# One of sixteen states is scaled by C on GpSimd and summed on TensorE, in a state-space layer with a routed feed-forward part

## What is computed

```python
u     = conv4(h) + conv_b                      # causal, per channel
dt, Bm, Cm = split(u @ xproj_w.T)              # 128, 16 and 16 columns
delta = softplus(dt @ dtproj_w.T + dtproj_b)
h_n[t] = exp(delta[t] * A_n) * h_n[t-1] + delta[t] * Bm[t, n] * u[t]
y[t]   = sum_n h_n[t] * Cm[t, n] + u[t] * D_skip
x1     = x + ga * y
```

## Time and profile before

| | |
|---|---|
| median of 3 runs | 1313.03 us (1310.49 to 1315.65) |
| the profiled execution | 1310.42 us, of which the span is 1308.7 us |
| PE busy | 1120.7 us, 86% of the span |
| DVE busy | 1110.2 us, 85% |
| POOL busy | 916.8 us, 70% |
| ACT busy | 877.6 us, 67% |
| granted PE clock, mean | 0.929 of full speed |

### The profile page before, as it was taken

How to read it: one execution, slowest core, us unless ns; L and a number is a source line. 1 busy time by engine, 2 the same in 40 slices (tenths; PEclk the granted TensorE clock), 3 DMA queues, 4 the chain that set the end, 5 groups by cost and what they waited for, 6 DMA issues and landing times. The chain is left out here.

```text
span 1308.7 us, 19847 instructions
## 1 busy us (share of the span) xinstructions
PE 1120.7 (86%) x5556; PEld 753.5 (58%) x5556; DVE 1110.2 (85%) x1562; ACT 877.6 (67%) x1684; POOL 916.8 (70%) x788
## 2 busy tenths in 40 slices
PE   8979778767769988898889998989889698999994
PEld 4467655445546656565557674656566465666551
DVE  4898899999988999899789998999889998853145
ACT  4864887948658975897598669976788474453231
POOL 2576686788778878888898767988887877423211
PEclk9999969757979999999999998999999789999997
DMA  6576443123224325233444521442541345785575
GB/s 213 182 262 218 121 158 101 49 73 139 82 93 121 129 66 153 94 130 96 140 119 132 145 64 60 143 137 72 155 121 66 115 143 183 232 285 185 153 232 171
DMA packets 104739, 181.02 MB, mean 138 GB/s; under 512 B 24864, under 2 KB 33056, under 8 KB 103608
## 3 DMA queue, kind: packets, MB, share of 16 engines
q1 hardware_dynamic: 91432, 141.33, 35.2%
q0 software_dynamic: 13200, 38.43, 7.7%
HBM read 116.34 MB, written 68.86 MB: 142 GB/s over the span
## 5 line engine op out<-in xcount | busy, mean ns | idle before, releaser
L1247 POOL TENSOR_TENSOR DB<-DU,BR 128x1024 f32<-128x1024 f32 x222 | 523.3, 2365 | 125.2 <-DVE H L1677 107.8
L2014 PE MATMUL pb<-ID,H 128*128 128x128 f32 x2048 | 323.8, 294 | 86.8 <-DVE ACC L1702 63.5
L1465 ACT ACTIVATE pb<-DELP,AN 128x512 f32<-128x512 f32 x448 | 305.7, 687 | 135.5 <-DVE H L1677 127.0
L1702 DVE SCALAR_TENSOR_TENSOR ACC<-pb,CTM,ACC 128x512 f32<-128x512 f32 x512 | 373.5, 730 | 13.9 <-PE pb L2014 13.4
L2014 PEld LDWEIGHTS pb<-ID,H 128*128 128x128 f32 x2048 | 254.2, 151 | 173.5 <-DVE ACC L1702 67.6
L1677 DVE TENSOR_TENSOR_SCAN H<-pb,DB 128x512 f32<-128x512 f32 x256 | 310.9, 1215 | 35.1 <-ACT pb L1465 17.3
L1677 DVE TENSOR_TENSOR_SCAN H<-pb,ST,DB 128x512 f32<-128x512 f32 x192 | 244.9, 1275 | 12.4 <-ACT pb L1465 9.1
L1232 POOL DMA_INDIRECT ydr<-YO,SCR x85 | 89.9, 1058 | 145.6 <-ACT YO L1547 129.7
L1547 ACT ACTIVATE YO<-pb,SCR 128x512 f32<-128x512 f32 x85 | 58.1, 683 | 71.5 <-PE pb L2117 71.1
L2087 PE MATMUL pb<-WU,XTS 128*128 x340 | 99.5, 417 | 0.0
L2112 PE MATMUL pb<-WD,GT 128*128 x170 | 98.4, 661 | 0.0
(11 more groups left out here) (251 smaller groups left out, 1731.9 us busy)
## 6 DMA issues: line engine op xcount, KB each, us to landing
BR<-bscr SPq DMA_DIRECT2D x112, 256.0 KB
XS<-xdr SPq DMA_DIRECT2D x85, 256.0 KB
DU<-ydr SPq DMA_DIRECT2D x64, 256.0 KB
xdr<-ZZ SPq DMA_DIRECT2D x37, 264.0 KB, 5.3
ACC<-in_x SPq DMA_DIRECT2D x16, 512.0 KB, 3.5
DU<-in_x SPq DMA_DIRECT2D x7, 1024.0 KB, 5.6
x1s<-ACC SPq DMA_DIRECT2D x24, 256.0 KB, 2.2
DELP<-x1s SPq DMA_DIRECT2D x24, 256.0 KB, 3.5
```

The lines of the kernel that those rows point to most:

```text
L1247: eng.tensor_tensor(DB[:, i % NDB:i % NDB + 2], DU[:, c % 2, r:r + 2], BR[:, n % 2:n % 2 + 1].to_broadcast([128, 2, CT]), ALU.mult).then_i ...
L1465: eng.activation(DA[i % NDA][:], DEL[:, c % 2, r], ACT.Exp, scale=AN[:, r, n:n + 1]).then_inc(S["da"], 1)
L1702: eng.scalar_tensor_tensor(out=acc, in0=banks[bank_of["flip", c, n, r]][:], scalar=1.0 if n < 0 else CTM[:, c % 2, j, st:st + 1], in1=acc, ...
L2014: t = eng.transpose(b[:, dt * 128:dt * 128 + 128], src[:, dt, r * 128:r * 128 + 128], ID[:])
```

## The change

In the chunks 1 to 6 the state 1 no longer goes through its own four flips and four accs. Instead the row of C for that state is written to HBM (`cw`, 512 single elements) and read back as a broadcast row CR (`cr`); POOL multiplies the state in H by it, in two instructions of 128x1024 (`hs`); and each of the four flips of the skip term becomes eight matrix products with the identity, four of U and four of the scaled state, added in the PSUM bank. The four accs of the skip term then add both. The skip flips of these chunks wait for both `hs`, and the scan of state 4 now waits for the last skip flip.

The expert rows' places XS go from 4 to 3, which gives the room for CR. The back phase gets four pairs of places for the rows and eight for x1; the new ones lie where chunk 7 has its own DU and DEL, and are free only when chunk 7 has made its last use of them. The acc of state 0 now also waits for the second half of the accumulator's load (`d_xa1`).

The tables PLACES and BANKS are replaced as a whole. The numbers that matter below, before and after: the skip flips of chunk c at 2048c+104 to 2048c+127, then at 2048c+327 to 2048c+430 (chunk 7 as before), and the skip accs at 2048c+121 to 2048c+144, then at 2048c+373 to 2048c+493; the new `hs` at 2048c+201 to +272 in the chunks 1, 2, 3 and 5 and at 2048c+312 and +333 in the chunks 4 and 6; `gbk` (five small POOL instructions on GBC) at 1106, then -30, just ahead of the dbu of slot 2; the load of the second half of ACC for chunk 6 at 12166, then 12440 (its first acc has 12530); of the expert tiles' `dn`, 40 have numbers below 14336 (chunk 7) before and 39 after, of the `up` 44 and 42, of the `xt` 46 and 42.

```diff
+FOLD = (1,)
...
-NXS = 4
+NXS = 3
...
+def folded(c, n):
+
+    return n in FOLD and c > 0 and c not in SPLIT
+
+
+def folding(c):
+
+    return folded(c, FOLD[0])
...
+    for c in filter(folding, range(NC)):
+        at += [("cw", c)] + [("cr", c, n) for n in FOLD] + [("hs", c, n, r) for n in FOLD for r in (0, 2)]
...
-        at += [(32 * s, ("scan", *unit(s))), (32 * (s + LAG) + 1, ("flip", *unit(s))), (32 * (s + LAG) + 50, ("acc", *unit(s)))]
+        at.append((32 * s, ("scan", *unit(s))))
+        if not folded(*unit(s)[0:2]):
+            at += [(32 * (s + LAG) + 1, ("flip", *unit(s))), (32 * (s + LAG) + 50, ("acc", *unit(s)))]
...
+        CR = sb("CR", [128, len(FOLD), CT])
...
+        cscr = nc.dram_tensor("cscr", [NC, len(FOLD), CT], f32).ap()
...
+        def x1_chunk(r):
+
+            return NC - 2 if r < 4 else NC - 1
+
+        def z_chunk(r):
+
+            return NC - 2 if r < 2 else NC - 1
+
         def x1_tile(g, t):
 
             cs, j = tokens(g)[t]
             if not bounced(cs):
                 return acc_tile(cs // 2, 2 * (cs % 2) + j)
-            return DEL[:, (NC - 2) % 2, back_no(g, t) % 4]
+            r = back_no(g, t) % 8
+            return DEL[:, x1_chunk(r) % 2, r % 4]
 
         def z_tile(g, t, way):
 
-            return DU[:, (NC - 2) % 2, 2 * (back_no(g, t) % 2) + way]
+            r = back_no(g, t) % 4
+            return DU[:, z_chunk(r) % 2, 2 * (r % 2) + way]
 
 
         def turn_of_z(g, t):
 
-            return S[f"d_g{back_no(g, t) % 2}"], back_no(g, t) // 2
+            return S[f"d_g{back_no(g, t) % 4}"], back_no(g, t) // 4
 
 
         def turn_of(g, t):
 
             r = back_no(g, t)
-            return S[f"d_v{r % 4}"], S[f"d_p{r % 4}"], r // 4
+            return S[f"d_p{r % 8}"], sum(32 if x < 4 * (NC - 2) else 16 for x in range(r % 8, r, 8))
...
+                elif what == "cw":
+                    c = k[0]
+                    eng.wait_ge(S["bct"], c + 1)
+                    eng.wait_ge(S["dts"], c + 1)
+                    for i, n in enumerate(FOLD):
+                        eng.dma_start(cscr[c, i].rearrange("(j p) -> p j", p=128), CTM[:, c % 2, :, n],
+                                      allow_slow_non_contiguous=True).then_inc(S["d_cw"], 16)
+                elif what == "cr":
+                    c, n = k
+                    i = FOLD.index(n)
+                    eng.wait_ge(S["d_cw"], 16 * len(FOLD) * c)
+                    if c > 1:
+                        eng.wait_ge(S["hs"], 2 * (len(FOLD) * (c - 2) + i + 1))
+                    eng.dma_start(CR[:, i], cscr[c, i:i + 1, :].to_broadcast([128, CT])).then_inc(S["d_cr"], 16)
...
-                        eng.wait_ge(S["fin"], b - 1)
+                        eng.wait_ge(S["fin"], b - 3)
                     elif way == 0:
-                        eng.wait_ge(S["dbu"], slot(NC - 2, NS - 1, 3) + 1)
+                        eng.wait_ge(S["dbu"], slot(z_chunk(b), NS - 1, 3) + 1)
...
-                    loaded, stored, turn = turn_of(g, t)
-                    if turn:
-                        eng.wait_ge(stored, 16 * turn)
+                    moved, before = turn_of(g, t)
+                    if before:
+                        eng.wait_ge(moved, before)
                     else:
-                        eng.wait_ge(S["da"], slot(NC - 2, NS - 1, 3) + 1)
+                        eng.wait_ge(S["da"], slot(x1_chunk(back_no(g, t)), NS - 1, 3) + 1)
                     eng.wait_ge(S[f"d_x1{2 * (cs % 2) + j}"], 16 * (cs // 2 + 1))
-                    eng.dma_start(x1_tile(g, t), x1s[rows_of(g, t), :]).then_inc(loaded, 16)
+                    eng.dma_start(x1_tile(g, t), x1s[rows_of(g, t), :]).then_inc(moved, 16)
...
+                elif what == "hs":
+                    c, n, r = k
+                    i = FOLD.index(n)
+                    eng.wait_ge(S["scan"], slot(c, n, r + 1) + 1)
+                    if state_kept(c, n):
+                        eng.wait_ge(S["st"], nth["st", c, n])
+                    eng.wait_ge(S["d_cr"], 16 * (len(FOLD) * (c - 1) + i + 1))
+                    h = H[:, (c * NS + n) % NH, r:r + 2]
+                    eng.tensor_tensor(h, h, CR[:, i:i + 1].to_broadcast([128, 2, CT]), ALU.mult).then_inc(S["hs"], 1)
...
-                        eng.wait_ge(S["flip"], nth["flip", pc, pn, 3])
+                        eng.wait_ge(S["flip"], nth["flip", pc, -1, SKIP[-1]] if folded(pc, pn) else nth["flip", pc, pn, 3])
...
+                        eng.wait_ge(S["d_xa1"], 16 * (c + 1))
...
+                    if n < 0 and r == 2 and folding(c):
+                        eng.wait_ge(S["hs"], 2 * len(FOLD) * c)
                     b = work_bank(eng, task)
                     src = U if n < 0 else H[:, (c * NS + n) % NH]
-                    for dt in range(4):
+                    parts = [U] + [H[:, (c * NS + x) % NH] for x in FOLD] if n < 0 and folding(c) else []
+                    for dt in range(4 if parts else 0):
+                        for x, part_of in enumerate(parts):
+                            t = eng.matmul(b[:, dt * 128:dt * 128 + 128], part_of[:, dt, r * 128:r * 128 + 128], ID[:],
+                                           start=x == 0, stop=x == len(parts) - 1)
+                    for dt in range(0 if parts else 4):
                         t = eng.transpose(b[:, dt * 128:dt * 128 + 128], src[:, dt, r * 128:r * 128 + 128], ID[:])
```

More of the change, by code:

```diff
@@ L38 @@
 PLACES = {
-        "del": (11, 17, 1852, 1865, 1916, 1942, 3384, 3394, 3516, 3529, 5944, 5954, 6008, 6018, 7995, 8005, 8077, 8131, 9973,
[5 rows of a table removed]
[L45 to L50, removed]
-        "bdh": (147,),
[L52 to L57, removed]
@@ L230 @@
-        "out": (15832, 15864, 16023, 16166, 16413, 16479, 16541, 16606, 16750, 16839, 16928, 17036, 17144, 17267, 17346, 17472,
[5 rows of a table removed]
+        "del": (-3, -2, 1852, 1865, 1938, 1979, 3706, 3714, 3738, 3853, 6005, 6012, 6018, 6025, 8050, 8056, 8074, 8080, 10101,
[5 rows of a table added]
+        "gbt": (176,),
+        "gbm": (11,),
+        "gbk": (-30,),
+        "gbb": (1233,),
+        "gbe": (1274,),
+        "gbs": (1340,),
+        "bdh": (147,),
+        "bdl": (176,),
+        "gbl": (1507, 1514, 16610, 17638),
+        "dg2": (12,),
@@ new lines @@
+        "rowz": (227, 242),
+        "rowy": (231, 235, 238, 246, 249, 253),
+        "rcq": (237, 314),
+        "rt": (1260, 1270),
+        "mod": (1295, 1296),
+        "ldw": (315, 326, 499, 643, 782, 939, 1103, 1301),
[7 rows of a table added]
+        "skx": (174, 178, 180, 182),
+        "skp": (184, 186, 188, 190),
+        "skc": (115, 137, 142, 156),
+        "flip_": (2387, 2413, 2445, 2471, 4453, 4476, 4499, 4522, 6496, 6524, 6547, 6570, 8566, 8585, 8603, 8622, 10567, 10589,
+        10616, 10667, 12654, 12675, 12695, 12716, 14440, 14447, 14454, 14458),
@@ new lines @@
+        13805, 13812, 13818),
+        "bct": (1389, 3033, 5581, 7571, 9485, 11637, 13844),
+        "ct": (1413, 3062, 5605, 7569, 9457, 11661, 13860),
+        "ctm": (1421, 3055, 5613, 7597, 9517, 11661, 13869),
+        "dtp": (1420, 3143, 5614, 7591, 9543, 11688, 13866),
+        "dtq": (1425, 1430, 1435, 3149, 3156, 3162, 5619, 5623, 5628, 7597, 7604, 7610, 9549, 9556, 9562, 11694, 11700, 11706,
+        13869, 13873, 13877),
+        "dts": (1450, 3156, 5652, 7636, 9578, 11723, 13908),
+        "dtr": (1482, 3188, 5680, 7692, 9610, 11768, 13915),
@@ new lines @@
+        "yst": (6333, 6671, 6735, 6799, 6860, 7115, 7243, 7819, 8335, 8468, 8780, 8791, 8847, 9100, 9679, 9743, 9807, 10200,
[12 rows of a table added]
+        "fin": (15812, 15813, 16259, 16262, 16381, 16394, 16418, 16479, 16644, 16715, 16787, 16841, 16966, 17056, 17146, 17225,
+        17848, 17891, 17937, 17973, 18071, 18135, 18188, 18278, 18368, 18421, 18493, 18583, 18655, 18726, 18899, 18935),
+        "out": (15917, 15921, 16433, 16465, 16837, 16856, 16876, 16909, 17082, 17149, 17221, 17274, 17400, 17490, 17584, 17659,
[5 rows of a table added]
@@ L254 @@
[L254 to L263 removed]
+    "rt": "46562",
+    "tr": "52453234636644226663464464366646",
+    "dtp": "22346342",
@@ L264 @@
+    "cpe": "3546222244343433633224646622",
+    "skx": "2564",
+    "dtr": "4346322",
+    "ftr": "22334364266423426446424333343632",
+    "r1": "3334244243636462",
+    "r2": "3334246232334464",
+    "hb": "23332334642423346664632663422463",
+    "rk": "264363422",
+    "xt": "3363363622442332334664333364362664666344333366263346624433433636346664364234234234346",
+    "gt": "34466323643624266644426442234442646436662623",
 }
@@ L1011, in _ @@
                     eng.wait_ge(S["fin"], back_no(g, t) + 1)
-                    eng.dma_start(out[rows_of(g, t), :], x1_tile(g, t)).then_inc(turn_of(g, t)[1], 16)
+                    eng.dma_start(out[rows_of(g, t), :], x1_tile(g, t)).then_inc(turn_of(g, t)[0], 16)
             for g in range(len(GROUPS)):
                 for t in range(len(tokens(g))):
-                    _, stored, turn = turn_of(g, t)
```

(7 more changed lines are left out.)

126 lines of the change are left out of this document (48 added, 78 removed), and 260 rows, old and new, of the table PLACES.

## The result

The kernel after takes 1342.32 us (median of 4 runs, 1339.38 to 1346.18), the kernel before 1311.88 us beside it on the same chip: ratio 1.0231, 95% interval 1.0207 to 1.0255. The profiled execution has a span of 1340.2 us against 1308.7.

A forecast was written before the change was run, and what follows sets the result against it. The prediction took DVE to bound chunks 1 to 6 and summed -15.4 + 6.1 + 0.7 + 0.5 + 1.0 - 0.8 = -7.9 us, giving 1302.5 us for the profiled execution and 1305 us for a median, range 1291 to 1322.

The forecast's parts named there:

- What bounds the kernel: Claimed chunks 1 to 6 go at DVE's pace, chunk 7 has DVE and PE near the limit, then PE bounds.
- The accs removed: Chunks 1 to 6: 24 accs fewer on DVE at 0.64 us each, -15.4 us.
- The matrix products: PE in chunks 1 to 6: products and transposes equal in number, taken as 0, between -7.5 us and 0.
- hs on GpSimd: Twelve POOL multiplications of 2.365 us in chunks 1 to 6 delay dbus and scans: +6.1 us, bounds 0 and 28.4.
- The port rule: DVE and POOL locking each other out over SBUF: by the rows, more POOL work costs DVE's scans and accs nothing.
- CR: SP waiting at cr for cw to land, 0 to about 1.2 us each: cost 0, upper bound 2.4 us.
- gbk and the load of ACC: Moved steps: gbk before the first scans +0.7 us (0 to 4), chunk 6's accumulator load +0.5 us (0 to 3).
- Chunk 7 and after: About 10 us more PE work arrives there, covered by 22.3 us of PE idle time in chunk 7: +1 us.
- TensorE takes it back: Rival: PE sets the finish from chunk 7 on, 10 us more work isn't hidden; 1314 us, no change. Chance 0.18.
- XS and the back phase: Three places for expert rows cost 0; additional back-phase places take about 0.8 us off the final chain.
- The order: Rewritten order shifting a chunk by more than a few us: named as a failure sign the rows can't price.
- GpSimd becomes the bound: Rival: POOL has no lead early in each chunk, every hs delays dbu and scan; +13.0 us, 1326 us. Chance 0.15.

The follow-up runs named there:

- e16: Kernel before with the 24 accs of state 1 in chunks 1 to 6 cut from 512 to 8 columns; 1313.83 us, 0.9986 of before.
- e12: Kernel before with each skip transpose of chunks 1 to 6 made two products of U with ID, about 32 us more TensorE work; 1344.51 us, 1.0265 of before.
- e3: Kernel after with each hs multiplication on GpSimd cut from 1024 to 8 elements a partition; 1334.01 us, 1.0147 of before.
- e13: Kernel after with its skip products replaced by plain transposes of U, state 1 left out of the sum; 1334.28 us, 1.017 of before.
- e14: Kernel after with skip products replaced by transposes of U and each hs cut to 8 elements a partition; 1327.52 us, 1.0136 of before.
- e8: Kernel after with cr issued some 220 to 300 numbers (14 to 20 us) later; 1338.29 us, 1.0183 of before.
- e1: Kernel after without the fold: rewritten order and banks, three XS places, skip steps mostly at the numbers of before; 1338.2 us, 1.0187 of before.
- e2: Kernel before with three XS places in place of four, nothing else changed; 1312.67 us, 0.9995 of before.
- e18: Kernel before with both cuts: 24 accs of state 1 to 8 columns and 288 transposes left out in chunks 1 to 6; 1312.8 us, 0.9981 of before.
- e17: Kernel before without three of every four transposes of states 1, 5, 9 and 13 in chunks 1 to 6; 1313.08 us, 0.9995 of before.

## Why the prediction was wrong, step by step

**What bounds the kernel** is the step that failed. "These chunks go at DVE's pace" was read from busy shares of 97, 91 and 89% and from three lines in the order of time. e16 takes DVE's work away and the time stays, with 11.1 us more of scans waiting for ScalarE and GpSimd; e12 adds work to PE, at 86 to 95% in chunks 3 to 6, and there it comes out whole. In chunk 4 DVE was idle 12.9 us, five times what four accs take. Busy shares this close, on four engines that go through fixed orders and wait for each other's banks and buffers, name no bound. Less work for VectorE gave next to nothing here; work added to TensorE came out.

**The accs removed**, -15.4 us: VectorE did lose 16.1 us of busy time after. In the kernel before, 10.7 us less busy time are worth 1.8 us (e16; by its interval between 4.3 faster and 0.7 slower).

**The matrix products**, 0 with bounds of -7.5 and 0: mis-sized, and of the wrong sign. "line 1936, is 3.8 us busy for 32, 0.119 us each" took 32 records for 32 products; the code there issues 4 tiles x 4 = 16. By that row a product is 0.238 us, twice what was taken. A folded chunk has 32 products at 0.222 in place of 32 transposes at 0.11, 3.6 us more, 21.5 us in six. "In chunks that go at DVE's pace neither end moves the finish" then hid it. Taking the products out of after, for plain transposes of U, gave 8.0 us (1.0231 to 1.017). The Trainium skill has rules on this in two places ("Perfetto Trace Analysis", Transposes: use a transpose, not a standard matmul, for what is logically one; "TensorE: Matmul & The Clock Gate", Terms: transpose mode is four times as fast in float32). The trace agrees on the direction and measures a factor of two.

**hs on GpSimd**, +6.1 us: the size of one was right (2.360 us). Its cost is 11 us by e3 and 4.5 by e13 to e14. The forecast lies between; of the waits of DVE for DB 23.7 us are seen after, 17.0 before. The prediction's sign "PE waits for hs at the skip flips" is in the trace once, for 7.2 us.

**The port rule** of the Trainium skill ("SBUF — State Buffer", the shared port pair): judged rightly by the rows. Accs take 728 ns and scans 1212, before 730 and 1214, though POOL is busy 28 us more.

**CR**, 0 with 2.4 at most: SyncE was held 24.9 us in 5 waits, not 0 to 1.2 each. The bounds were those of landing times of contiguous rows; `cw` gathers single elements and took up to 7.2 us beyond the issue of `cr`. Worth some 4 to 6 us (e8), if all that e8 gained is SyncE's wait.

**gbk and the load of ACC**, +1.2: the first scan starts 3.0 us later, chunk 0 is 6.6 us shorter, chunk 6 1.1 longer. Not tested apart.

**Chunk 7 and after**, +1 with 10 us of work arriving: the amount was right, 10.3 us of busy time, perhaps in part by luck, since the clock behind the scans was lower too; the cover did not exist. Idle time of PE from chunk 7 on was 47.1, 47.2 and 47.7 us in before, e1 and after. It was no reserve. That it is made of waits which come with each tile is my reading and not shown. This was the rival "TensorE takes it back", right in mechanism and price, as one part of a larger loss.

**XS and the back phase**, 0 and -0.8: the places are right, e2 shows 0.9995. The stretch without PE work at the end is 14.2 us, from 16.2, somewhat more than the 0.8.

**The order**, priced at nothing except for single steps, is the largest term: 1.9 to 2.3% with the accs and without the fold, 1.4% with neither products nor hs (e14, which still has cw and cr). It is the order together with its banks; no run has this order with the banks of before. The prediction named it last, as what "these rows can't price", and gave it no chance. Chunk 7 is 14 us of e1's 31 (305.1 against 291.3 us of PE work); chunks 1 to 6 are 22 more (823.4 against 801.1 us), and the start and chunk 0 give 5 back.

As ratios, taken out one after the other: 0.6% products (e13), 0.3% hs (e14) and 1.4% for the order and what hangs on it are the 2.3%. Taken out first, hs is 0.8% (e3), so the parts are not independent. The rival "GpSimd becomes the bound" had the sign, not the cause. None of these versions beats the kernel before.

**What stays open**: what in the order or banks costs in chunks 1 to 6, why the fold in the old order costs 3%, and what keeps e18 from being faster. The lower clock is one part that the rows show; whether the time stayed because of it, or whether something else kept the pace, no run tells apart. A mere change of banks changes the time by more than any term of the sum.

## What to carry to other kernels

Before a busy share is called a bound, take away the work in question and time it: here 10.7 us less for VectorE gave 0.14%. Read the busy time of that run as well: 32 us of TensorE's work taken away lowered its busy time by 11.5 us and the time by 0.05%. In a kernel whose order and banks were fitted together, price a change by what it displaces, and run the new order without the change and the new banks without the new order; either moved this time by more than the change could bring. Count records against what the code issues before dividing a busy time by them.

## What the hardware showed that was not expected

A float32 product with the identity is two instructions, 0.222 us, a transpose of the same tile one, 0.11 us. Leaving out matrix work lowered TensorE's granted clock: 0.909 to 0.914 in the ten runs of e17, where the kernel before beside it has a mean of 0.925, and 0.910 to 0.916 in e13 against 0.919 to 0.929 in after. More work (e12) left it at 0.921 to 0.930, with a mean of 0.927 in the kernel before beside it. Other PSUM banks for the same instructions in the same order cost 1.6 and 4.2%. SyncE's queue waited up to 7.2 us, 24.9 us in five waits, for a transfer that gathers 512 elements of 4 bytes.
